# The gate of a gated feed-forward: a sigmoid on ScalarE and a product of three on VectorE, against one Silu on ScalarE, woven between the steps of a recurrence

## What is computed

```python
# x: 2 x 1024 x 512, f32
u = layernorm(x) @ W_in.T + b_in                      # 512 -> 1024
s_t = tanh(u_t + s_{t-1} * gamma + beta)              # 1024 steps in time, one after the other
x = x + layernorm(states @ W_out.T + b_out)           # 1024 -> 512
h = layernorm(x)                                      # weights below rounded to float8 e4m3fn, used in f32
gate = silu((h @ gate_w) * gate_scale)                # 512 -> 1536
up = (h @ up_w) * up_scale
x = x + layernorm(((gate * up) @ down_w) * down_scale)  # 1536 -> 512
```

## Time and profile before

| | |
|---|---|
| median of 3 runs | 625.39 us (625.18 to 625.69) |
| the profiled execution | 625.78 us, of which the span from the first instruction to the last is 624.0 us |
| granted TensorE clock, mean over the span | 0.937 of full speed |
| PE busy | 528.8 us, 85% |
| DVE busy | 481.0 us, 77% |
| ACT busy | 310.6 us, 50% |
| POOL busy | 240.4 us, 39% |

### The profile page before, as it was taken

How to read it: one execution, slowest core, us unless ns; L and a number is a source line. 1 busy time by engine, 2 the same in 40 slices (tenths; PEclk the granted TensorE clock), 3 DMA queues, 4 the chain that set the end, 5 groups by cost and what they waited for, 6 DMA issues and landing times.

```text
span 624.0 us, 9844 instructions
## 1 busy us (share of the span) xinstructions
PE 528.8 (85%) x2880; PEld 449.0 (72%) x2880; DVE 481.0 (77%) x1832; ACT 310.6 (50%) x1442; POOL 240.4 (39%) x320
## 2 busy tenths in 40 slices
PE   4655232878999999999999999999999992999993
PEld 4644211568977998789878987799779971798992
DVE  4999997999778667966787679767886678675734
ACT  1354423365554755576546654665466544452330
POOL 2776672555224222422333332422342224243532
PEclk9957757789999999999999999999999996999997
DMA  7453440301010200110012001100001000100000
GB/s 235 128 171 123 124 141 29 90 29 52 1 35 1 69 1 1 35 67 2 1 34 69 1 2 34 56 14 0 2 3 65 2 0 2 67 2 2 1 35 34
DMA packets 16598, 27.47 MB, mean 44 GB/s; under 512 B 2336, under 2 KB 4512, under 8 KB 16544
## 3 DMA queue, kind: packets, MB, share of 16 engines
q1 hardware_dynamic: 16544, 26.84, 13.7%
HBM read 22.63 MB, written 4.19 MB: 43 GB/s over the span
## 4 chain that ended last, share of the span: by engine, by line
DVE 57%; ACT 21%; PE 14%; issue 3%; DMA 1%; SPq 1%; POOL 1%; POOLq 0%; DVEq 0%; ACTq 0%
DVE recur L634 23%; ACT pairs L922 10%; PE gate_up L528 7%; ACT pairs L909 4%; DVE fused L728 4%; ACT sigm L942 4%; DVE gated L721 3%; PE wide L553 3%; DVE peaks L780 3%; ACT fused_hi L957 3%; PE wide L493 2%; DVE rounder_own L776 2%; DVE y L675 2%; DVE z L793 2%; DVE x_in L658 2%
## 5 line engine op out<-in xcount | busy, mean ns | idle before, releaser
L922 ACT ACTIVATE pairs<-recur 128x16 f32<-128x16 f32 x1024 | 191.2, 187 | 249.5 <-DVE recur L634 247.1
L634 DVE TENSOR_TENSOR_SCAN recur<-recur,pairs 128x32 f32<-128x32 f32 x1024 | 234.4, 229 | 101.5 <-ACT pairs L922 100.1
L1025 POOL TENSOR_TENSOR fused_lo<-fused,fused_hi 128x256 fp32r<-128x256 f32 x96 | 71.1, 741 | 180.5 <-ACT fused_hi L957 180.4
L468 PE MATMUL wide<-x_norm_t,w_in_sb 128*128 128x256 f32 x448 | 106.6, 396 | 17.5 <-ACT pairs L909 13.2
L482 PE MATMUL wide<-w_out_sb,pairs 128*128 128x512 f32 x224 | 101.3, 606 | 22.1 <-DMA w_out_sb<-w_out_t 22.1
L468 PEld LDWEIGHTS wide<-x_norm_t,w_in_sb 128*128 128x128 f32 x448 | 87.6, 199 | 34.6 <-ACT pairs L909 15.4
L482 PEld LDWEIGHTS wide<-w_out_sb,pairs 128*128 128x128 f32 x224 | 65.5, 297 | 51.8 <-DMA w_out_sb<-w_out_t 22.5
L528 PE MATMUL gate_up<-x_hi,gate_q 128*128 128x256 f32 x384 | 96.8, 285 | 1.0 <-DVE fused L728 0.6
L528 PE MATMUL gate_up<-x_lo,up_q 128*128 128x256 f32 x384 | 96.0, 283 | 0.0
L528 PE MATMUL gate_up<-x_hi,up_q 128*128 128x256 f32 x384 | 95.6, 282 | 0.0
L528 PE MATMUL gate_up<-x_lo,gate_q 128*128 128x256 f32 x384 | 94.9, 281 | 0.0
(11 more groups left out here) (75 smaller groups left out, 640.2 us busy)
## 6 DMA issues: line engine op xcount, KB each, us to landing
x_in<-x SPq DMA_DIRECT2D x16, 256.0 KB, 3.1
x_res<-x SPq DMA_DIRECT2D x16, 256.0 KB, 3.1
out<-z SPq DMA_DIRECT2D x14, 256.0 KB, 2.4
raw_own<-gate_w SPq DMA_DIRECT2D x10, 256.0 KB, 2.8
raw_own<-down_w SPq DMA_DIRECT2D x9, 256.0 KB, 2.7
w_in_sb<-w_in_t SPq DMA_DIRECT2D x4, 512.0 KB, 6.8
raw_own<-up_w SPq DMA_DIRECT2D x8, 256.0 KB, 2.7
w_out_sb<-w_out_t SPq DMA_DIRECT2D x8, 256.0 KB, 2.9
```

The source lines that it names most:

```text
L468: ins = eng.matmul(wide[bank][:, jj * TOK:(jj + 1) * TOK], w_in_sb[:, k, j * P:(j + 1) * P], x_norm_t[:, k, :], start=(k == 0), stop=(k == ...
L634: eng.tensor_tensor_scan(preact[:, part(h), :].rearrange("p c k -> p (c k)"), factors[:, part(h), :].rearrange("p c k -> p (c k)"), pairs[ ...
L922: eng.activation(pairs[:, (n * T + t) % RING, part(h), 0], preact[:, part(h), 1], ACT.Tanh).then_inc(s_state[h], 1)
L1025: eng.tensor_tensor(fused_lo[:, f, :], fused[:, f, :], fused_hi[:, f, :].bitcast(F32), ALU.subtract).then_inc(s_fused_lo, 1)
```

## The change

The sigmoid on ACT becomes one Silu of the scaled gate, which writes `gated` directly; the product L721 on DVE, the buffer `sigm` and its semaphore go. A chunk has three places instead of four. The up product moves to the place of the former gate product, one slot earlier, and the high part (and with it the low part) moves one slot earlier too. In code without the recurrence the up product stays at +1.2 and the high part moves from +2.4 to +2.2. `taken` now counts one slot of DVE for a chunk instead of two, so the rounding of the last weight pieces in block 1 moves into slots that came free. The warm-up activation, ahead of which the activation table is loaded, is a Silu too.

```diff
-REST = {"next_to_last": (0, 2, 3, 5), "last": (4, 6, 7, 8), "down": 24}
+REST = {"next_to_last": (0, 2, 4), "last": (4, 6, 7), "down": 24}
...
-END_USE = ((0, 0.3, 0.4, 1), (2, 2.3, 2.4, 3))
+END_USE = ((0, 0.3, 1), (2, 2.3, 3))
...
             c = int(place + 4.7)
-            found[i] = (c, c + 2, c + 3, c + (5 if i < LAG else 4))
+            found[i] = (c, c + 2, c + (4 if i < LAG else 3))
         else:
             c = place + GATE_UP_PLACES
-            found[i] = (c, c + 1.2, c + 1.4, c + 2.4)
+            found[i] = (c, c + 1.2, c + 2.2)
...
             for places in use.values():
-                at |= set(places[1:3])
+                at.add(places[1])
...
-            def gates(n, use):
-                for i, (_, gate_at, up_at, _) in use.items():
+            def fuse(n, use):
+                for i, (_, up_at, _) in use.items():
+                    yield up_at
                     chunk = KI * n + i
                     g, f = i % NG, i % NF
-                    yield gate_at
                     if chunk == 0:
                         eng.wait_ge(s_scales_in, 32)
-                    eng.wait_ge(s_sigm, chunk + 1)
-                    eng.scalar_tensor_tensor(out=gated[:, f, :], in0=gate_up[g][:, 0, :],
-                                             scalar=gate_scale_cols[:, i:i + 1], in1=sigm[:, f, :], op0=ALU.mult,
-                                             op1=ALU.mult).then_inc(s_gated, 1)
-                    yield up_at
                     eng.wait_ge(s_gated, chunk + 1)
...
-                eng.activation(warm[:, 0:1], warm[:, 1:2], ACT.Sigmoid)
+                eng.activation(warm[:, 0:1], warm[:, 1:2], ACT.Silu)
...
-            def sigmoids(n, use):
-                for i, (sigmoid_at, _, _, _) in use.items():
-                    yield sigmoid_at
+            def gates(n, use):
+                for i, (gate_at, _, _) in use.items():
+                    yield gate_at
+                    if n == 0 and i == 0:
+                        eng.wait_ge(s_scales_in, 32)
                     eng.wait_ge(s_gate_up, KI * n + i + 1)
-                    eng.activation(sigm[:, i % NF, :], gate_up[i % NG][:, 0, :], ACT.Sigmoid,
-                                   scale=gate_scale_cols[:, i:i + 1]).then_inc(s_sigm, 1)
+                    eng.activation(gated[:, i % NF, :], gate_up[i % NG][:, 0, :], ACT.Silu,
+                                   scale=gate_scale_cols[:, i:i + 1]).then_inc(s_gated, 1)
```

More of the change, by code:

```diff
@@ L176, in recurrent_sandwich_kernel @@
         NF = 3
-        sigm = sb("sigm", [P, NF, TOK])
         gated = sb("gated", [P, NF, TOK])
@@ L246, in recurrent_sandwich_kernel @@
         s_gate_up = sem("s_gate_up")
-        s_sigm = sem("s_sigm")
         s_gated = sem("s_gated")
@@ L829, in _ @@
                 if n >= 2:
-                    strands.append(gates(n - 2, {KI - 2: REST["next_to_last"], KI - 1: REST["last"]}))
+                    strands.append(fuse(n - 2, {KI - 2: REST["next_to_last"], KI - 1: REST["last"]}))
                     strands += tail(n - 2, TAIL)
@@ L840, in _ @@
                     if n < LAST:
-                        strands.append(gates(n - 1, use_places(FFN, 0, IN_TIME - 1)))
+                        strands.append(fuse(n - 1, use_places(FFN, 0, IN_TIME - 1)))
                     else:
-                        strands.append(gates(n - 1, use_places(LAST_FFN, 0, LAST_CHUNKS - len(END_USE))))
+                        strands.append(fuse(n - 1, use_places(LAST_FFN, 0, LAST_CHUNKS - len(END_USE))))
                         strands += residual_norm(LAST, 0, GROUP_AFTER)
@@ L853, in _ @@
             end_use = dict(enumerate(END_USE, LAST_CHUNKS - len(END_USE)))
-            weave(gates(LAST - 1, {**end_use, **use_places(END_FFN, LAST_CHUNKS, KI, beside=False)}),
+            weave(fuse(LAST - 1, {**end_use, **use_places(END_FFN, LAST_CHUNKS, KI, beside=False)}),
                   *tail(LAST - 1, END_TAIL), *residual_norm(LAST, 1, GROUP_AFTER),
                   *[split_x1(LAST, g, GROUP_AFTER["t2_high"][g]) for g in range(GROUPS)],
-                  gates(LAST, use_places(GROUP_FFN, 0, KI, beside=False)))
+                  fuse(LAST, use_places(GROUP_FFN, 0, KI, beside=False)))
             weave(*tail(LAST, GROUP_TAIL), add_last_residual())
@@ L936, in split_x1 @@
                              wide[bank][:, halves(half)].rearrange("p (k t) -> p k t", t=P)).then_inc(s_x1_hi, 1)
-            def sigmoids(n, use):
-                for i, (sigmoid_at, _, _, _) in use.items():
-                    yield sigmoid_at
+            def gates(n, use):
[3 more added lines that the diff above has]
+                        eng.wait_ge(s_scales_in, 32)
                     eng.wait_ge(s_gate_up, KI * n + i + 1)
-                    eng.activation(sigm[:, i % NF, :], gate_up[i % NG][:, 0, :], ACT.Sigmoid,
-                                   scale=gate_scale_cols[:, i:i + 1]).then_inc(s_sigm, 1)
+                    eng.activation(gated[:, i % NF, :], gate_up[i % NG][:, 0, :], ACT.Silu,
+                                   scale=gate_scale_cols[:, i:i + 1]).then_inc(s_gated, 1)
             def high_parts(n, use):
-                for i, (_, _, _, high_at) in use.items():
+                for i, (_, _, high_at) in use.items():
                     yield high_at
@@ L963, in _ @@
                     use = {KI - 2: REST["next_to_last"], KI - 1: REST["last"]}
-                    strands += [sigmoids(n - 2, use), high_parts(n - 2, use)]
+                    strands += [gates(n - 2, use), high_parts(n - 2, use)]
                 if n < LAST:
@@ L975, in _ @@
                         use = use_places(LAST_FFN, 0, LAST_CHUNKS - len(END_USE))
-                    strands += [sigmoids(n - 1, use), high_parts(n - 1, use)]
+                    strands += [gates(n - 1, use), high_parts(n - 1, use)]
                 weave(*strands)
@@ L980, in _ @@
             last_use = use_places(GROUP_FFN, 0, KI, beside=False)
-            weave(sigmoids(LAST - 1, use), high_parts(LAST - 1, use),
+            weave(gates(LAST - 1, use), high_parts(LAST - 1, use),
                   *[split_x1(LAST, g, GROUP_AFTER["t2_high"][g]) for g in range(GROUPS)],
-                  sigmoids(LAST, last_use), high_parts(LAST, last_use))
+                  gates(LAST, last_use), high_parts(LAST, last_use))
         @block.gpsimd
```

## The result

The changed kernel takes 627.1 us in the median of 13 runs (626.28 to 627.83), the kernel before 625.39 us in the median of its 13 (625.08 to 625.84): ratio 1.0026, 95% interval [1.0019, 1.0033]. It is slower by 1.7 us where 3.2 were forecast, so it lies inside the predicted range of 626.0 to 631.5, nearer to its lower end than to the 628.6 forecast. A second set on another occasion gave 627.93 against 625.48, slower by 2.5 us, ratio 1.0042 [1.0029, 1.0055].

A forecast was written before the change was run, and what follows sets the result against it. The recurrence's step (scan, wait, tanh, wait) was taken to set the pace up to block 7, then PE. Terms -1.9 + 4.4 + 0.7 + 0.2 - 0.2 = +3.2 us gave 628.6 us, range 626.0 to 631.5.

The forecast's parts named there:

- The doubled slots: 18 slots of blocks 1 to 7 where ACT holds gate and high part between two tanhs: 0.246 us each, +4.4 us.
- Doubled slots are free: Rival: on ACT the cast starts in the Silu's shadow without delaying the tanh, so only gains stay, 624.0 us; chance 8%.
- The product: One DVE product fewer per chunk in the recurrence: 72 that count, at 0.027 us each, -1.9 us.
- Block 1: Moved-up weight rounding makes DVE operations stretch beside POOL's in block 1: 1.5 us in sum, +0.7 us net.
- The end of the recurrence: Block 7, slot 62 to last tanh: two slots gain a second operation, seven products go; 0.30 less 0.06 slack, +0.2 us.
- The end of the program: Last low part on POOL is ready 0.53 us earlier, of which PE can use only 0.24: -0.2 us.
- PE as the ceiling: PE busy 63.92 of 64.67 us in a middle block, so a block's gains must stay below a few tenths.
- The table load: Rival: Silu and tanh share no table, so 79 gates between steps need two loads each, +202 us, 828 us; chance 1%.

The follow-up runs named there:

- e2: Kernel before, sigmoid and both products kept, with only the high parts of chunks 0, 1, 2 and 10 one slot earlier: 631.1 us against 626.0.
- e5: Changed kernel with chunk 2's high part moved beside chunk 3's gate, a fourth such shared slot in each block: 629.96 us against 625.48 for the kernel before.
- e4: Changed kernel with block 1's weight rounding pieces back in their former slots: 628.26 us against 626.0 for the kernel before.
- e1: Changed kernel with the high parts back in their former slots, so none shares a slot with a gate: 624.02 us against 626.0 for the kernel before.
- e7: Kernel before with the Silu alone, chunk 0's gate one slot later and DVE's scaling of z in slots 49 and 50: 616.21 us against 625.48.

## Why the prediction was right, and which of its sizes were off

**The doubled slots** were forecast at 0.246 us each, 18 of them, +4.4. They cost 0.743 - 0.485 = 0.258 in after, 0.257 in e2 and 0.28 in e5: 18 x 0.258 = +4.6. Mechanism, places and size held. "Doubled slots are free" is refuted by e2, in which nothing else was changed.

**The product** was forecast at 0.027 us, -1.9 in sum. This is the term that was most mis-sized: "with one gone I take half". A pair costs 1.510 - 3 x 0.484 = 0.058 us over plain steps, one product 1.473 - 1.452 = 0.021. So removing one gives back 0.037, not half of 0.05: 72 x 0.037 = -2.7. What follows a single 0.46 us operation mostly catches up (0.472 behind it), what follows a first of two can't, because the second stands there. I had also read the 1.50 from one place, to 0.01 us, where the mean is 1.510.

**Steps that stretch for no shown reason** were not in the sum. In all three executions of the kernel before, step 0 of block 5 takes 0.82 us (0.54 in the other blocks), step 58 of block 2 takes 0.62 (0.48) and step 83 of block 5 takes 0.64 to 0.65 (0.52): 0.54 us. None of the three does so in any of the three executions of after. After has another, step 52 of block 4, 0.66 us where 0.48 stood, but it costs nothing: the step behind it, DVE's collision with POOL in slot 53, is as much shorter (1.29 against 1.47). The trace has an "issue" wait of 0.16 us on ACT in two of the three, as in this timeline of ACT in block 5 of the kernel before:

```profile
409.51 0.41 ACT L957 CAST fused_hi<-fused 128x256 fp32r<-128x256 f32 x1 [0.16 <-issue]
```

They belong to a place in a program and move when instructions are added or removed. Their difference is worth -0.5 us here. Together, 15 x 0.258 - 60 x 0.037 - 0.54 = +1.1, against 326.05 - 324.87 = +1.18 measured for blocks 2 to 6. They are also why block 5 did not become longer (65.40 against 65.46 us), while blocks 3, 4 and 6 did by 0.33 to 0.36, near the 0.4 forecast for each. What causes them was not tried, but the traces' DMA packets say where they stand. In blocks 2 to 7 of the thirteen profiles ACT and DVE have 29 "issue" waits in all, and 0.64 to 0.80 us behind the start of the delayed operation each time a packet of the kind "instruction" starts. Step 0 of block 5, whose wait has another name, has one too, 0.66 to 0.93 us behind its late tanh. That points at the loading of the next instructions.

**Block 1** was forecast at +0.7 net for the rounding. In pairs that agree in step 65 block 1 became 0.68 (70.57 against 69.89) and 0.75 us (71.18 against 70.43) longer, and steps account for it: the two doubled slots +0.52, ten products -0.37, and the rounding. The timelines of POOL and DVE show the rounding in after, answering to the earlier trace rows:

```profile
149.63 1.32 POOL L1050 TENSOR_TENSOR down_q<-raw_own,rounder_own 128x512 fp32r<-128x512 f32 x1
150.90 1.79 POOL L1020 TENSOR_TENSOR fused_lo<-fused,fused_hi 128x256 fp32r<-128x256 f32 x2
```

```profile
150.21 1.03 DVE L777 TENSOR_SCALAR z<-z 128x512 f32<-128x512 f32 x1
...
151.29 0.81 DVE L786 TENSOR_TENSOR z<-z 128x256 f32<-128x256 f32 x1
...
152.66 0.40 DVE L786 TENSOR_TENSOR z<-z 128x256 f32<-128x256 f32 x1
...
153.62 0.79 DVE L792 TENSOR_TENSOR down_q<-z 128x256 fp32r<-128x256 f32 x1
```

Three steps are stretched, 1.08, 0.86 and 0.86 us where 0.52, 0.48 and 0.48 stood, +1.3 in all, and the two of 0.87 and 0.88 that the earlier trace rows belong to are gone, -0.8: +0.5, where I had 1.5 - 0.8. DVE's 1.03 us operation, 0.41 by itself, starts 0.58 us behind POOL's and ends 0.29 after it (151.24 against 150.95). That the move of the rounding is the cause has to be put more carefully than I did: by e4 and e1 it is the rounding on DVE against the low parts on POOL, and moving either of them alone costs as much or more.

**The end of the recurrence** was forecast at +0.30 less 0.06 of slack. From slot 64 of block 7 to the last scan it became 31.58 - 31.08 = 0.50 us longer (31.6 against 31.1 in the other executions too). Two doubled slots less seven products are 0.52 - 0.26; the rest is step 111 of block 7, 0.71 us in all three executions of after and 0.48 in all three of before. It is a collision that the forecast had not: POOL's low part, one slot earlier now, starts 0.29 us ahead of a DVE operation in front of which it used to be 0.20 us late (552.14 and 552.34 in the kernel before). Timelines of POOL and DVE:

```profile
552.54 0.79 POOL L1020 TENSOR_TENSOR fused_lo<-fused,fused_hi 128x256 fp32r<-128x256 f32 x1 [1.06 <-ACT fused_hi L952]
```

```profile
552.83 0.65 DVE L684 TENSOR_SCALAR x_norm<-x_res,mean_var_r,rstd_r 128x256 f32<-128x256 f32 x1
```

With the low parts back where they were, in e1, the step takes 0.48 us again; in e4 and e5 it takes 0.71 to 0.72. That the end came out near the forecast, 0.4 against 0.2 us, is so in part by chance. PE, which had no wait at this place, now has one for the last tanh (timeline of PE):

```profile
561.18 1.23 PE L491 MATMUL wide<-w_out_sb,pairs 128*128 128x512 f32 x2 [0.43 <-ACT pairs L915]
```

**The end of the program** was forecast at -0.2. The last low part still starts 2.10 us behind the one before, but PE no longer waits for it (timelines of PE and POOL, answering to the earlier trace rows):

```profile
612.83 0.39 PE L551 MATMUL wide<-down_q,fused_lo 128*128 128x512 f32 x1
613.07 0.39 PE L551 MATMUL wide<-down_q,fused_hi 128*128 128x512 f32 x1
613.29 0.39 PE L551 MATMUL wide<-down_q,fused_lo 128*128 128x512 f32 x1
```

```profile
612.46 0.73 POOL L1020 TENSOR_TENSOR fused_lo<-fused,fused_hi 128x256 fp32r<-128x256 f32 x1 [2.10 <-ACT fused_hi L952]
```

The matmuls follow at 0.22 to 0.24 us throughout. From the start of the last output projection to that of the last matmul it takes 614.23 - 561.18 = 53.05 us, before 613.67 - 560.36 = 53.31: -0.26.

**The sum** with the measured sizes is 4.6 - 2.7 - 0.5 + 0.5 + 0.4 - 0.3 = +2.0 us, against 1.7 and 2.5 us in the two measurements. Of the 1.2 us that the forecast was too high, 0.8 is the product, 0.5 the stretched steps, 0.2 the rounding and 0.1 the program's end; the doubled slots and the recurrence's end were each 0.2 too low. Nearly all of the error went one way, so the range was not met by errors that cancelled.

**PE as the ceiling** was wrong in the prediction, though the sum did not need it. It let a block gain only "those few tenths of PE" by which 64.67 us exceed 63.92. Block 4 of e7 takes 63.31 us, 1.4 less than before, and PE has no wait in it.

**The table load:** one, as before, and a Silu at 469 ns between tanhs; no switch takes place. The Trainium skill ("ScalarE: Activation LUTs", what ACT_TABLE_LOAD costs) says that an ACTIVATE runs at one element per cycle and lane for every function; this trace agrees as far as the two functions go, 469 ns for both.

**Where the gain went.** The removed work was 44 us of DVE that stood in slots with room, so it was worth 2.7 us in steps. The closer places took 4.6 us, on an engine that is half idle.

## What to carry to other kernels

In a loop in which two engines hand a small result back and forth, the free time of a step is one operation of a certain length on each engine, and work is priced by how far it goes beyond that: here an operation of 0.39 us on DVE was free, one of 0.46 cost 0.02, two of them in neighbouring slots 0.06, and two operations in the same slot on ACT 0.26. When an operation disappears, look in the order for what now falls into the same slot before moving the rest up: the Silu by itself gained 0.4%, and the slot that was saved behind it cost 0.7%. And search the busy engine's timeline for single operations that take a multiple of their usual time: six of them, moved four slots ahead, gave 5.7 us, twice what the Silu by itself gives.

## What the runs showed of the hardware that was not expected

A busy share near 1 hid room: PE counted 63.92 us for the matmuls of a block in the kernel before and 63.31 for the same ones in e7, so the first number was no lower bound for the block.

The same program showed a granted clock of 0.50 at 133 to 135 us in some executions and 1.00 in others, with 0.56 us between them in block 1; which one is not set by the kernel, since both kernels showed both.

Steps at fixed places of a program stretch by 0.1 to 0.3 us in every execution, most with an "issue" wait of 0.15 to 0.20 us in the trace, and others do so when the program is edited elsewhere. An edit of a few instructions gained some 0.5 us in this way here. A packet that loads instructions starts 0.64 to 0.80 us behind each such wait; that the loading is the cause was not tested.

DVE's operation of 0.39 us took 1.41 when it started 0.01 us behind a POOL operation of 1.27. The Trainium skill ("SBUF — State Buffer", on the engine side of SBUF) has the port pair of the two as a lock for a whole instruction, which would be up to 1.27 + 0.39 = 1.66 us; the 1.41 is nearer to that than to a sharing, and e7 shows that the step's excess of 0.93 us goes when the two are apart.

The other collisions say it more sharply. In the profiles of before and after, 63 DVE operations that take 0.39 to 0.42 us otherwise began while a POOL operation was running and took at least 1.4 times as long. POOL had begun 0.01 to 1.01 us ahead of them, and each ended at a fixed distance behind POOL's end: 0.15 us for those of 0.39, 0.28 to 0.29 for those of 0.41. So a collision costs what is left of POOL's operation, not a share of it: in step 111 of block 7, 0.79 - 0.29 + 0.15 = 0.65 us.
